# Third layer of a four-layer network on one core: two convolution blocks as folded matmuls, compact reciprocals, and a recurrence that takes two heads in one matmul

## The reference

```
q = causal_conv_silu(normed @ Wq, conv_q)   # 4 taps per channel, then silu
k = causal_conv_silu(normed @ Wk, conv_k)
v = causal_conv_silu(normed @ Wv, conv_v)   # 256 channels
q = l2norm(q.reshape(B, T, H, HK)) * HK ** (-0.5)   # 4 heads of 32
k = l2norm(k.reshape(B, T, H, HK))
def _step(S, inp):                          # S: 32 x 64 per head
    S = S * jnp.exp(g_t)[..., None, None]
    v_eff = (v_t - jnp.einsum('bhk,bhkv->bhv', k_t, S)) * b_t[..., None]
    S = S + k_t[..., None] * v_eff[..., None, :]
    o_t = jnp.einsum('bhk,bhkv->bhv', q_t, S)
```

## Time and profile before

| What | Value |
|---|---|
| Time, median of 3 runs | 4452.48 us (4449.95 to 4452.6) |
| The profiled execution's own time | 4490.13 us |
| Its span | 4487.8 us |
| TensorE busy, mean granted clock | 3583.8 us (80%), 0.865 |
| VectorE, ScalarE, GpSimd busy | 2576.2, 2008.9, 1248.7 us |
| conv phase, barrier to barrier | about 2761 to 2886 us |
| unit phase | about 2886 to 2963 us |
| recur phase | about 3314 to 3432 us |

### The profile page before, as it was taken

How to read it: one execution, slowest core, us unless ns; L and a number is a source line. 1 busy time by engine, 2 the same in 40 slices (tenths; PEclk the granted TensorE clock), 3 DMA queues, 4 the chain that set the end, 5 groups by cost and what they waited for, 6 DMA issues and landing times. The chain is left out here.

```text
span 4487.8 us, 92926 instructions
## 1 busy us (share of the span) xinstructions
PE 3583.8 (80%) x30644; PEld 2181.0 (49%) x30644; DVE 2576.2 (57%) x5821; ACT 2008.9 (45%) x3927; POOL 1248.7 (28%) x1828
## 2 busy tenths in 40 slices
PE   4699999749995799942999963457976289999997
PEld 2244444337772122220677731147975256666664
DVE  5577677541115677745677755744833556666664
ACT  5366666413335477721333342222322256556652
POOL 0111111100000111100677732603524334444440
PEclk9799999859996799965999975567768589999999
DMA  4322222100002211100665511011001333333330
GB/s 110 73 54 59 54 57 56 28 10 5 10 5 58 45 47 45 38 3 15 178 159 159 159 41 52 28 58 35 3 3 32 47 110 114 118 116 112 119 113 25
DMA packets 197624, 286.63 MB, mean 64 GB/s; under 512 B 40609, under 2 KB 154728, under 8 KB 196978
## 3 DMA queue, kind: packets, MB, share of 16 engines
q1 hardware_dynamic: 193270, 274.87, 21.7%
q0 software_dynamic: 4096, 8.40, 1.1%
HBM read 229.14 MB, written 35.72 MB: 59 GB/s over the span
## 5 line engine op out<-in xcount | busy, mean ns | idle before, releaser
L704 ACT ACTIVATE att_E<-att_pX,att_gs 128x512 f32<-128x512 f32 (+3 forms) x1024 | 722.5, 740 | 413.4 <-PE att_pX L638 177.3
L741 DVE TENSOR_REDUCE att_mx<-att_pS 128x1 f32<-128x512 f32 (+4 forms) x960 | 730.3, 787 | 290.6 <-PE att_pS L612 186.4
L1888 POOL TENSOR_TENSOR att_E<-att_E,att_rz 128x128 f32<-128x128 f32 (+3 forms) x512 | 357.6, 719 | 436.4 <-DVE att_rz L2096 436.4
L607 PE MATMUL att_pS<-att_ks,att_qs 72*128 72x512 bf16 (+4 forms) x1536 | 410.1, 339 | 80.9 <-DMA att_ks<-parts 57.4
L632 PE MATMUL att_pX<-att_qs,att_ks 75*128 75x512 bf16 (+4 forms) x1536 | 422.4, 330 | 29.9 <-ACT att_E L704 15.0
L1598 POOL TENSOR_TENSOR pairs_h<-pairs_m,pairs_r 128x512 f32<-128x512 f32 x272 | 346.3, 1273 | 355.5 <-DVE pairs_m L1661 348.1
L1622 PEld LDWEIGHTS pairs_po<-pairs_a,pairs_h 128*128 128x128 f32 x2176 | 286.2, 192 | 129.6 <-issue 129.1
L570 POOL CAST att_mp<-att_m 16x128 bf16<-16x128 f32 x288 | 80.4, 279 | 942.9 <-DVE att_m L752 917.7
L649 PE MATMUL att_pO<-att_E,att_vs 128*9 128x512 f32 (+3 forms) x3072 | 323.0, 492 | 1.3 <-ACT att_E L704 1.3
L1643 ACT ACTIVATE pairs_r<-pairs_ph 128x512 f32<-128x512 f32 x272 | 162.5, 597 | 330.1 <-PE pairs_ph L1614 330.1
L2027 ACT ACTIVATE att_E<-att_S,att_nm 128x128 f32<-128x128 f32 (+3 forms) x512 | 281.9, 556 | 38.6 <-DVE att_nm L2090 38.5
(11 more groups left out here) (413 smaller groups left out, 6661.8 us busy)
## 6 DMA issues: line engine op xcount, KB each, us to landing
pairs_c<-weights SPq DMA_DIRECT2D x272, 256.0 KB, 3.8
att_bias<-in_bias_dram SPq DMA_DIRECT2D x64, 896.0 KB, 4.5
parts<-proj_part SPq DMA_DIRECT2D x144, 128.0 KB, 2.3
att_xb<-xnT SPq DMA_DIRECT2D x64, 256.0 KB, 2.7
att_qs<-parts SPq DMA_DIRECT2D x192, 64.0 KB
att_ks<-parts SPq DMA_DIRECT2D x192, 64.0 KB
att_w<-in_w3a_dram SPq DMA_DIRECT2D x64, 192.0 KB, 2.4
att_qs<-parts SPq DMA_DIRECT2D x96, 96.0 KB
```

The lines of the kernel that those rows point to most:

```text
L607: ins = nc.tensor.matmul(pS[:, bank, n * w:(n + 1) * w], qs[:K1, u, x, q * P:(q + 1) * P], ks[:K1, u, x, :w], start=(n == 0 or not causal) ...
L704: nc.scalar.activation(E[:, kt % 2, WIDE * xp:WIDE * (xp + 1), :w], places(c)[0], ACT.Exp, scale=gs[:, g % 2, gain_of:gain_of + 1]).then_i ...
L741: V.reduce_max(dst, src, AX.X).then_inc(s_mx, 1)
L1888: nc.gpsimd.tensor_tensor(E[:, k, :width(j)], E[:, k, :width(j)], rz[:, u, k:k + 1].broadcast_to([P, width(j)]), ALU.mult).then_inc(s_n, 1)
```

## The change

It touches three phases.

1. `conv`: the four taps of q and k are folded into their projection. VectorE multiplies four copies of the taps (a new table `folds2`, 512 KB) with the weights, two blocks of 128 x 512 (`scale`), and TensorE adds four matmuls in PSUM for each q or k block, each on tokens shifted by one. ScalarE's silu reads the sum there. v keeps its four passes on VectorE. The order is written out: one v block and one q or k block per turn, 16 turns.
2. `unit`: ScalarE squares; one matmul per block gathers the sums of its four heads into 4 of 32 rows, 8 blocks into one tile of 32 x 512, so that there are two roots and two reciprocals in all. 16 matmuls spread the results back to 128 rows, and VectorE multiplies out of PSUM.
3. `recur`: `st` holds each left-hand block twice, with a mask (`own`) that leaves the even heads in one copy and the odd heads in the other, so that one 64 x 64 matmul does two heads: 80 in a step. GpSimd makes its copies as products with the mask, ScalarE with a scale. VectorE takes over the copy of the second group's output (`leave`). All 8 bodies are written out instead of the loop.

The diff, cut to its core:

```
+                def folded(e):
+                    x, m, o = seq(R.xn2T, e // 2), e % 2, pq[:, e % 2]
+                    if e < 2:
+                        pe.wait_ge(s_fold, e + 1)
+                    if e >= 2:
+                        pe.wait_ge(s_qk, e - 1)
+                    for n in reversed(range(NTAP)):
+                        late = NTAP - 1 - n
+                        ins = nc.tensor.matmul(o[:, late:], fold[:, m, n], x[:, :T - late], start=(late == 0), stop=(late == NTAP - 1))
+                    ins.then_inc(s_mq, 1)
+                for c in range(NV):
+                    value(c)
+                    folded(c)
...
+                copy(0)
+                for c in range(NV):
+                    if c:
+                        silu(c - 1)
+                    if c + 1 < NV:
+                        copy(c + 1)
+                    silu_qk(c)
...
+                for c in range(NV):
+                    aside(pool, c)
+                    pool.wait_ge(s_turn, c + 1)
...
+                for h in range(PARTS):
+                    for n in range(PER):
+                        square(h * PER + n)
+                    root(h)
...
+                for h in range(PARTS):
+                    inverse(h)
+                for n in range(N):
+                    dve.wait_ge(s_B, n + 1)
+                    nc.vector.tensor_tensor(part(n), pB[:, n % 4], part(n), ALU.mult).then_inc(s_un, 1)
...
-                            ins = nc.gpsimd.tensor_copy(st[:, n, m], seqs(src, g, i * 2 + cc))
+                            ins = nc.gpsimd.tensor_tensor(st[:, n, m], both(seqs(src, g, i * 2 + cc)), mine, ALU.mult)
...
-                        for h in range(H2):
-                            r = slice(h * 32, h * 32 + 32)
-                            ins = nc.tensor.matmul(dst[r, b], lhs[r, b], rhs[r, b], start=True, stop=True)
+                        for h in range(2):
+                            r = slice(h * HP, (h + 1) * HP)
+                            ins = nc.tensor.matmul(dst[r, b], wide(lhs[r, b]), rhs[r, b], start=True, stop=True)
...
-                        ins = nc.scalar.activation(st[:, n % IT, m], seqs(src, g, i * 2 + cc + (n // IT) * 2), ACT.Copy)
+                        for a in range(2):
+                            ins = nc.scalar.activation(st[:, n % IT, m, :, a], seqs(src, g, i * 2 + cc + (n // IT) * 2), ACT.Copy, scale=own[:, a:a + 1])
...
+                        if not begin:
+                            leave(at, i, cc, 1)
...
-                run_bodies(pe, NBODY, body)
+                for i in range(NBODY):
+                    body(i, i == 0, i == NBODY - 1)
```

More of the change, by code:

```diff
@@ L2217, in _, with value @@
                 pe.wait_ge(s_w, 32)
[L2219 to L2227, removed]
+                def value(c):
+                    if c >= 2:
+                        pe.wait_ge(s_raw, c - 1)
+                    nc.tensor.matmul(pv[:, c % 2], ws[:, 2 + c % 2], seq(R.xn2T, c // 2), start=True, stop=True).then_inc(s_mv, 1)
@@ L2248, in body, with copy @@
[L2248 to L2257, removed]
+                def copy(c):
+                    act.wait_ge(s_mv, c + 1)
+                    if c >= 2:
+                        act.wait_ge(s_conv, c - 1)
+                    nc.scalar.activation(raw[:, c % 2, PAD:], pv[:, c % 2], ACT.Copy).then_inc(s_raw, 1)
@@ L2275, in conv @@
                     ins.then_inc(s_conv, 1)
[L2277 to L2294, removed]
@@ L2296, in _, with turn @@
[L2296 removed]
+                def turn(c):
+                    dve.wait_ge(s_silu, c + 1)
+                    if c >= 2:
+                        dve.wait_ge(s_v, c - 1)
+                    nc.vector.transpose(vt[:, c % 2], vy[:, c % 2]).then_inc(s_turn, 1)
+                dve.wait_ge(s_f, 16)
+                scale(0)
+                scale(1)
+                for c in range(NV):
+                    conv(c)
+                    if c:
+                        turn(c - 1)
@@ L2298, in _ @@
+                turn(NV - 1)
             @block.gpsimd
             def _(pool):
[L2300 to L2307, removed]
@@ L2324, in _ @@
             def _(sp):
[L2325 to L2340, removed]
+                sp.dma_start(to[:, :, :], gather).then_inc(s_to, 16)
@@ L2342, in _ @@
             @block.tensor
             def _(pe):
-                pe.wait_ge(s_c, 16)
-                def body(i, first, last):
-                    at = At(pe, i)
-                    for m in range(2):
-                        pe.wait_ge(s_sq, at(2, m + 1))
-                        if not first:
-                            pe.wait_ge(s_rt, at(2, m - 1))
-                        nc.tensor.matmul(ps[:, m], ones[:, :], sq[:, m], start=True, stop=True).then_inc(s_ss, 1)
-                run_bodies(pe, B, body)
@@ L2356, in _ @@
[L2356 to L2368 removed]
+                pe.wait_ge(s_to, 16)
@@ L2780, in body @@
                         dve.drain()
-                run_bodies(dve, NBODY, body)
+                    if last:
+                        leave(at, i, 2, 1)
+                for i in range(NBODY):
+                    body(i, i == 0, i == NBODY - 1)
 def output2_phase(nc, R, name, o, wg, nw, wo, xn, y_all, aside):
```

186 lines of the change are left out of this document (110 added, 76 removed).

## The result

| | Before | After |
|---|---|---|
| Median | 4451.22 us (4442.14 to 4452.6, 4 runs) | 4393.69 us (4387.06 to 4397.94, 4 runs) |
| The profiled execution's own time | 4490.13 us | 4387.06 us |
| Its span, granted clock | 4487.8 us, 0.865 | 4385.2 us, 0.882 |

The ratio is 0.9871 with a 95% interval of 0.9859 to 0.9883: 57.5 us faster (52 to 63), where 64 us were forecast. The two profiled executions differ by 103 us.

What follows compares the result with a forecast made beforehand. It took GpSimd and VectorE as nearly full in the convolution, VectorE last in the normalisation, TensorE at its own rate in the recurrence's later passes. Gains 9 + 34 + 21 = 64 us from 4452.5 gave 4388 us, range 4365 to 4416.

Steps and rivals of the forecast that it cites:

- What bounds the convolution: Convolution: GpSimd still needs 16 copies and 64 transfers and stays the limit; gain 9 us, 2 to 13.
- The turn: Convolution: GpSimd's turn of one copy and four transfers falls from 6.65 to 6.05 us, 15 turns 90.8 us.
- rival A: Convolution: TensorE becomes the bound; at 6.9 us a turn the phase loses 4 us, total 4401 us; chance 0.13.
- Normalisation: Unit phase: 39 to 44 us, taken as 42, against 76.4; gain 34 us, 28 to 38.
- the second reciprocal: Unit phase: transfer, gathers, waits, roots and this reciprocal of 3.35 us end 27 us into the phase.
- sixteen spread blocks: Unit phase: products paced by TensorE's spreading matmuls take 12.2 us, 17 at a slow start.
- Recurrence: Recurrence: 94 us from the first subtraction's old place to the last copy, against 114.5; gain 21 us, 8 to 26.
- The start: Recurrence: waiting for the mask and a first triple of products adds 3.0 us.
- the slow first step: Recurrence: the slow clock of the first 5 us adds 2.5 us.
- The step: Recurrence: 5.5 us a step, 5.15 to 6.3, with 160 records at 28.2 ns making 4.5 us.
- Fetch: Recurrence: new code costs 62 ns a matmul, 5.0 us a step, just hidden; old matmuls written out, 8 us a body.
- Rival B: Recurrence: held by GpSimd's products or by fetch, 6.3 us a step, gain 8, total 4401 us; chance 0.13.

Runs made afterwards that it cites:

- run 10: The change with the convolution's scatter transfers issued two turns earlier, twelve instead of four ahead of GpSimd's first copy: ratio 0.9859.
- run 2: The kernel before with the new convolution alone: ratio 0.998, 8.9 us gained.
- run 11: The change with twelve scatter transfers ahead of the first copy, two behind each copy, the last twenty in the normalisation: ratio 0.9821.
- run 8: The change with five extra matmuls filling TensorE's two waits in the normalisation: single execution without a ratio, phase 47 us.
- run 9: The change with the normalisation's spreading matmuls padded with zeros from 32 to 128 rows: single execution without a ratio, phase 39.5 us.
- run 12: The change with scatter transfers thinned out and partly moved into the normalisation, and spreading matmuls on 128 rows: ratio 0.9809, median 4395.86 us.
- run 5: The kernel before with its old recurrence written out as 8 bodies instead of first, loop of six, last: ratio 1.0082, 37 us slower.
- run 6: The change with its new recurrence put back into first body, loop of six, last body: ratio 0.9884.
- run 3: The kernel before with the new normalisation alone: ratio 0.9928, 32.0 us gained.
- run 1: The kernel before again, no edit, for a second profile: ratio 0.9995, 4478.0 us.

## Why the prediction came out, and where it did not

It gave 4388 us; the median was 4393.69, within the range. What bounds each stage was right in all three. That the stages of the two traces sum to 63.7 us, against 64 forecast, is partly luck: the convolution gave 3.8 us more than its term, the normalisation 3.0 and the recurrence 3.6 less, and 2.5 us came from stages that had no term. Point by point:

- **What bounds the convolution: right.** GpSimd, shown by run 10. The turn was 5.84 us instead of 6.05: the first four took 6.0 to 6.5 us, the next eight about 5.7, and the last three 5.5 to 5.6 nearly undisturbed, since the engines ahead were done but for the last turned block by 2850. The first copy came at 2777.80, 17 us into the phase as before. Gain 12.8 us by the trace for 9, 8.9 (4.9 to 12.9) by run 2.
- **TensorE in the convolution (rival A): refuted.** It had the fast clock from about 2772 to 2837 with 4.28 us a turn, and only the transfers kept it from setting the pace (run 11).
- **Normalisation: mechanism right, one term mis-sized.** Up to the end of the second reciprocal it took 23.3 us where I had 27. The sixteen spread blocks then took 22.2 us where I had 12.2, and 17 for a slow start. I had priced the slow clock as a matter of the start only; it fell at about 2895, before the second row of spreading matmuls, and stayed at 0.50 for 20 us of unbroken work. Runs 8, 9 and 12 tie that to the 32 rows. 45.5 us lie outside my 39 to 44, the gain of 31 us inside 28 to 38.
- **Recurrence: mechanism right, step mis-sized.** The start cost 2.3 us more (4.45 from the clearing of S to the first subtraction, 2.19 before) for 3.0, the slow first step 2.0 for 2.5. The step was 5.85 us for 5.5, which is 14 x 0.35 = 4.9 us; start, first step and end gave 1.7 of that back. Gain 17.4 for the 20.5 that the sum gives (written as 21). 5.51 us is the shortest step. In it TensorE has no idle row, but its groups don't close up: the 64 records of pO take 1.87 us, 29 ns each, as priced (28.2), while 32 records of pA, pU and pS take 1.24, 1.25 and 1.15 us from one start to the next, where 0.93 would do. That is 0.8 us a step for handing over to VectorE and ScalarE, for which I had 0.64. What fills the rest, 0.3 us a step, is open. In the loop it lies in front of pU, 0.2 to 0.4 us a time; written out, it comes in single stops of up to 0.5 us, 3 us of them in all. `Sg` is a part of it at most: the four steps with an `Sg` over 0.75 us took 5.78 to 6.49 us, but four with both at 0.5 or less took 6.03 to 6.21.
- **Fetch: right in both directions**, 8 us a body for old matmuls written out (37 us by the medians of run 5, 42 in its trace; five bodies pay it, where the prediction had six, since the loop's first pass was slow already) and nothing for the new ones (run 6). Rival B did not come: 5.85 is under 6.3.
- **Why 57.5 and not 64.** The stages of the traces do sum to 64. The profiled execution of the change is also the fastest of its four, 6.6 us under their median. So the sum holds for that execution; that the rest is the spread between executions fits the numbers, but no second profile of the change was taken to show it. I had also taken the 37.6 us by which the profiled execution of before stood above its median as harmless and spread out. It was VectorE's waits for rows in the output phase, 32.33 us the longest.
- A gain that I did not list: the experts behind the new normalisation took 109 us instead of 112 from their first load to their last addition, in the change and in run 3, and 111 in run 9. I have no cause for it.

## What to carry to other kernels

Where one engine has a free wait at the start of a phase and no gap later, moving independent work into that wait is worth nearly its length (9.6 of 11.0 us in run 10); then read which engine is next. When code is written out and executed once, count its instructions: it cost 37 us with 160 small matmuls in a 5.8 us step and nothing with 80. And before taking a profile's span as the base, look for the place that sets it above the median. Where three terms are off by 3 to 4 us each and their sum is right, the sum proves little; the stages have to be compared one by one.

## What the hardware showed unexpectedly

- Matmuls with 32 rows of weights kept TensorE full for 20.84 us without the clock rising from 0.50; the same with 128 rows, three quarters of them zeros, ran at 1.00 and took 10.57 us (run 9), and regained the clock after a wait that had cost it (run 12).
- A VectorE product of two SBUF inputs took up to 0.69 us instead of 0.41 beside plain copies on GpSimd, and 0.41 to 0.87 beside products.
- From the clearing of S to the end of the next layer's normalisation the old recurrence and what follows took 256 and 255 us in runs 2 and 3, 274 in run 1 and 290 in the first profile of before; the difference is VectorE's wait for a load of rows, up to 32 us at a time.
